# Graph attention and expert layers on one core: the attention's compares and masks run three units ahead of TensorE instead of four

## The reference

```python
seq = (layernorm(x) @ W_seq).reshape(N, H, DH)
score1, score2 = einsum(seq, a1), einsum(seq, a2)          # [H, N] each
scores = leaky_relu(score1[:, :, None] + score2[:, None, :], 0.2)
scores = scores + (1 - adj)[None] * -65500.0
hidden = einsum('hij,jhd->ihd', softmax(scores, -1), seq).reshape(N, 512)
x = x + elu(hidden @ W_out + b_out)
x = x + ffn(layernorm(x))       # shared FFN of 2048, 8 experts, 2 chosen per token
```

## Time and profile before

| | |
|---|---|
| median of 3 runs | 1058.4 us (1056.4 to 1060.9) |
| profiled execution, its own time | 1060.8 us |
| its span, first to last instruction | 1058.9 us |
| attention's units on TensorE | 99.8 to 487.9 us |
| mean granted TensorE clock | 0.983 of full speed |

### The profile page before, as it was taken

One profiled execution on the slowest core, in us unless ns is written; L12 is line 12 of the kernel. 1 busy time (PEld: TensorE's weight loads), 2 busy tenths in 40 slices (PEclk: granted clock), 3 DMA queues, 4 the chain that ended last, 5 costly groups with the idle time before them and its releaser, 6 DMA issues.

```text
span 1058.9 us, 27195 instructions
## 1 busy us (share of the span) xinstructions
PE 1006.7 (95%) x11256; PEld 890.0 (84%) x11256; DVE 803.9 (76%) x1197; ACT 666.5 (63%) x990; POOL 251.5 (24%) x271
## 2 busy tenths in 40 slices
PE   5996889999999999999899999999999999989998
PEld 4875889999999999997677888888888877778887
DVE  6776899999999999993699433448775668975554
ACT  2668999999989889933356333344454546655431
POOL 1103124334333443363331000000065000006500
PEclk9996999999999999999899999999999999999999
DMA  8781111111111111623635000020063124453242
GB/s 301 249 313 40 41 62 43 45 61 42 43 52 52 42 43 52 225 67 132 229 116 208 1 1 1 1 80 1 26 207 117 50 80 131 130 158 112 85 134 99
DMA packets 53778, 102.45 MB, mean 97 GB/s; under 512 B 6161, under 2 KB 26257, under 8 KB 53138
## 3 DMA queue, kind: packets, MB, share of 16 engines
q1 hardware_dynamic: 47666, 82.83, 23.6%
q0 software_dynamic: 3072, 8.39, 2.5%
q10 hardware_dynamic: 2928, 9.57, 2.4%
HBM read 74.69 MB, written 26.08 MB: 95 GB/s over the span
## 4 chain that ended last, share of the span: by engine, by line
PE 47%; issue 2%; DVE 2%; DMA 1%; POOL 1%; ACT 0%; SPq 0%; POOLq 0%; DVEq 0%; ACTq 0%
PE bank L1758 16%; PE bank L1291 16%; PE bank L668 3%; PE bank L1835 2%; PE bank L1786 1%; PE bank L1787 1%; PE bank L1789 1%; DMA xs<-sorted_latent_rows 1%; PE bank L1805 1%; PE bank L1779 1%; PE bank L1743 1%; PE bank L1741 1%; PE bank L665 1%; PE bank L1740 1%; DVE acc_rest L1492 0%
## 5 line engine op out<-in xcount | busy, mean ns | idle before, releaser
L730 ACT ACTIVATE arena<-arena 128x1024 fp8e4<-128x1024 f32 x320 | 336.6, 1136 | 2.5 <-ACT arena L722 1.6
L956 PE MATMUL bank<-arena 128*128 128x132 f16 x4096 | 285.6, 222 | 19.0 <-DVE arena L816 7.6
L956 PEld LDWEIGHTS bank<-arena 128*128 128x128 fp8e4 x4096 | 246.6, 98 | 20.8 <-issue 8.6
L1291 PE MATMUL bank<-xt,up_parts 128*128 128x512 f32 x768 | 186.2, 391 | 0.0
L1758 PE MATMUL bank<-down_parts,h_parts 128*128 128x512 f32 x768 | 184.5, 389 | 0.1
L960 PE MATMUL bank<-arena 128*128 128x66 f16 x4096 | 173.5, 196 | 0.0
L794 DVE TENSOR_SCALAR arena<-arena 128x1024 uint8<-128x1024 f32 x192 | 167.8, 940 | 2.7 <-DMA arena<-s_rows 2.7
L1758 PEld LDWEIGHTS bank<-down_parts,h_parts 128*128 128x128 f32 x768 | 143.9, 188 | 30.5 <-issue 0.5
L1291 PEld LDWEIGHTS bank<-xt,up_parts 128*128 128x128 f32 x768 | 142.3, 188 | 28.6 <-ACT relu_sb L1240 0.2
L960 PEld LDWEIGHTS bank<-arena 128*128 128x128 fp8e4 x4096 | 154.9, 98 | 0.0
L1265 DVE TENSOR_TENSOR relu_sb<-relu_sb 128x512 f32<-128x512 f32 x64 | 44.4, 693 | 118.0 <-ACT relu_sb L1240 110.9
(11 more groups left out here) (231 smaller groups left out, 1403.9 us busy)
## 6 DMA issues: line engine op xcount, KB each, us to landing
hid<-in_adjT SPq DMA_DIRECT2D x32, 512.0 KB, 5.8
arena<-s_rows SPq DMA_DIRECT2D x30, 512.0 KB, 3.7
sorted_latent_rows<-zeros SPq DMA_DIRECT2D x1, 4992.0 KB, 18.5
xs<-sorted_latent_rows SPq DMA_DIRECT2D x39, 128.0 KB, 2.1
sorted_expert_rows<-expert_y SPq DMA_DIRECT2D x39, 128.0 KB, 1.7
arena<-in_x SPq DMA_DIRECT2D x4, 1024.0 KB, 10.8
xr<-in_x SPq DMA_DIRECT2D x16, 256.0 KB, 2.8
up_sb<-in_upT ACTq DMA_DIRECT2D x1, 4096.0 KB, 14.0
```

Source lines behind the costliest of these rows:

```text
L730: last = nc.scalar.activation(m8[:, k, j, :], s1b[:, k % 2, :], ACT.Sigmoid, bias=bias_now[:, k % 2, j:j + 1], scale=STEEP, saturate=False)
L956: last = nc.tensor.matmul(o, m8[:, k, j, i * P:(i + 1) * P], vs[:, b, j, :], start=(j == 0), stop=(j == T - 1))
L1291: last = nc.tensor.matmul(bank[6 + s % 2][:, :], sa[:, s % 2, a, k, :], xt[c][:, b, k, :], start=(i == 0), stop=(i == len(mm) - 1))
```

## The change

`compare`, `mask_own` and `mask_acts` are called one unit closer to TensorE. In the slot of unit u, VectorE and ScalarE compare unit u + 3 and `mask_acts` is that of unit u + 2. Unit 3's compare, which was ahead of the loop, moves into slot 0, and the last pair's slots get the compare of unit 31 and the masks of units 30 and 31. GpSimd's wait on `m_ready` is lowered by one, so that it still means the end of VectorE's slot u - 1. The mask buffers stay four, and no instruction that computes is added or removed.

```diff
@@ ScalarE
                 def body(p, last):
                     for k in range(4):
-                        act.wait_ge(unit_in_psum, 4 * p + k + 1)
-                        if not last:
-                            if k >= 2:
-                                split_high(p + 1, k % 2)
-                            compare(p + 1, k)
+                        if not (last and k):
+                            act.wait_ge(unit_in_psum, 4 * p + k + 1)
+                        if not last and k >= 2:
+                            split_high(p + 1, k % 2)
+                        if not last or k == 0:
+                            compare(p + (k + 3) // 4, (k + 3) % 4)
...
                 compare(0, 2)
-                compare(0, 3)
                 with act.Fori(0, PAIRS - 1) as p:
                     body(p, False)
+                body(PAIRS - 1, True)
@@ VectorE
-                        if k or not first:
-                            dve.wait_ge(unit_in_psum, 4 * p + k + 1)
-                            collect(p, k)
-                        if not last:
-                            if k >= 2:
-                                low_values(p + 1, k % 2)
-                            compare(p + 1, k)
-                            mask_own(p + 1, k)
-
-                        if k == 0:
-                            mask_acts(p, 3)
-                        elif not last:
-                            mask_acts(p + 1, k - 1)
+                        dve.wait_ge(unit_in_psum, 4 * p + k + 1)
+                        collect(p, k)
+                        if not last and k >= 2:
+                            low_values(p + 1, k % 2)
+                        if not last or k == 0:
+                            compare(p + (k + 3) // 4, (k + 3) % 4)
+                            mask_own(p + (k + 3) // 4, (k + 3) % 4)
+                        if not last or k < 2:
+                            mask_acts(p + (k + 2) // 4, (k + 2) % 4)
...
                 mask_own(0, 2)
-                mask_acts(0, 2)
-                dve.wait_ge(unit_in_psum, 1)
-                collect(0, 0)
-                compare(0, 3)
-                mask_own(0, 3)
-                body(0, first=True)
-                with dve.Fori(1, PAIRS - 1) as p:
+                with dve.Fori(0, PAIRS - 1) as p:
                     body(p)
                 body(PAIRS - 1, last=True)
@@ GpSimd
-                        pool.wait_ge(m_ready, 4 * p + k + 3)
+                        pool.wait_ge(m_ready, 4 * p + k + 2)
                         pool.wait_ge(unit_in_psum, 4 * p + k + 1)
```

More of the change, by code:

```diff
@@ L831, in split_low, with body @@
                     nc.vector.tensor_scalar(ones_r[0:1, :], ident2[0:1, :], 0.0, 1.0, ALU.mult, ALU.add).then_inc(wo_low, 1)
-                def body(p, last=False, first=False):
+                def body(p, last=False):
                     for k in range(4):
```

## The result

The changed kernel takes 1075.5 us (median of 4 runs, 1073.7 to 1081.0) against 1059.7 us for the kernel before on the same chip (4 runs). The ratio is 1.016 with a 95% interval of 1.013 to 1.019: 16 us slower. The forecast was 1072.7 us, 14.3 us above before, in a range of 1065 to 1080. The single profiled executions say the same, with spans of 1074.8 and 1058.9 us. From the first matmul of unit 0 to the last `collect` the attention takes 504.12 - 99.31 = 404.8 us against 487.96 - 99.76 = 388.2, and from that `collect` to the end it is 570.7 us against 570.9. So the whole loss is in the attention.

The account below looks back on a forecast made before the run. VectorE was taken as the bound in the attention, TensorE 1% behind. Turns +10.8, start +3.5 and end 0 gave +14.3 us on 1058.4: 1072.7 us, own range 1066 to 1078, stated range 1065 to 1080.

Parts of the forecast that it names:

- The bound, and how much of the lead was left: Attention: VectorE bounds, TensorE 1% behind; masks are ready only 2.2 to 3.4 us before their unit starts.
- The turn as the sum of the larger of slot and unit: Four-slot attention turn: each slot costs the longer of VectorE's slot and TensorE's unit; 48.75 for 46.95 us, +10.8 in six.
- The start: First units of the attention: unit 2's mask comes later, unit 4 ends at 174.4 for 170.9; +3.5 us.
- The end: Behind unit 28: last slots and transposes before unit 31 stay hidden; 0 us, or 1 if it sticks out.
- ScalarE at no cost: Attention turns: ScalarE gets less slack, but its longest slot, 11.4 us, just fits in a unit; cost nothing.
- The clock: TensorE in the turns: priced at no loss; rival: a cold unit once a turn, +9 us, 1081.6 us, chance 0.07.
- The rivals of the slots: VectorE's slots: they even out (1063.4 us, chance 0.10) or GpSimd's interference goes (1056.7 us, chance 0.04).
- evening out: Rival, VectorE's slots become equally long: 1.5 us lost in all turns, with the start +5, 1063.4 us; chance 0.10.
- less interference: Rival, GpSimd's products run in VectorE's waits, compares shorten: turns -5.2, start +3.5, 1056.7 us; chance 0.04.
- the other side's mechanism: Not-slower rival: without GpSimd's interference all slots are under 11.8 us and TensorE runs without pause; 1056.7 us, chance 0.04.

Follow-up runs that it names:

- e3: Changed kernel with VectorE's mask of ScalarE's rows moved directly behind `collect`, ahead of low values and compare; 1063.4 us, 1.004 to the kernel before.
- e6: Changed kernel (lead of three) without GpSimd's multiplications for the values of pairs 1 to 7; 1059.9 us, 1.000 to the kernel before.
- e7: Kernel before (lead of four) without GpSimd's multiplications for the values of pairs 1 to 7; 1055.2 us, 0.995 to the kernel before.
- e5: Changed kernel, but in the first slot alone the mask of unit 2's ScalarE rows comes ahead of `collect`; 1073.7 us, 1.015 to the kernel before.
- e8: Changed kernel with one wait more: GpSimd's combine of unit 27 waits for the end of VectorE's slot 27; 1076.9 us (one run).
- e1: Changed kernel with ScalarE four units ahead as before, VectorE and GpSimd's count three ahead; 1079.4 us, 1.020 to the kernel before.
- e2: Kernel before with ScalarE alone three units ahead, VectorE and GpSimd unchanged; 1060.8 us, 1.002 to the kernel before.
- e11: e3 with the transposes behind unit 31's fifth token tile and GpSimd's slot released by the mask near the slot's start; 1071.6 us, 1.010 to before.

## Why the prediction was right

*The bound, and how much of the lead was left.* Right. What the chain of waits didn't say, the distance between mask and start did: 2.2 to 3.4 us were left of the lead, and a slot later was 7 us or more too late. e3 shows it from the other side, as the mask moved forward inside the slot brings the turn back without the fourth unit.

*The turn as the sum of the larger of slot and unit.* Predicted 48.75 us, measured 48.76. That they agree to 0.01 is luck: the two slots longer than a unit were 0.21 and 0.07 us shorter than forecast (11.84 for 12.05, 13.03 for 13.10), and the two that wait for TensorE took 11.95 and 11.94 us where a release was priced at 11.8. The waits were forecast as 1.43 and 0.37 us on VectorE and as 1.6 and 0.5 on TensorE; they are 1.63, 0.42, 1.77 and 0.6. e6, beside e7, agrees with the rule on other slots. Six turns give +10.9 us.

*The start.* Predicted +3.5 us, with unit 2 ready at 135.3, unit 4's release at 174.4; measured +3.6, with slot 4's start at 174.54 against unit 4's end at 170.9 before, and unit 0 0.45 us sooner. VectorE's timeline of the start in the changed kernel:

```profile
125.44 1.38 DVE L817 TENSOR_REDUCE arena<-bank 128x198 f32<-128x396 f32 x3
...
149.58 1.39 DVE L817 TENSOR_REDUCE arena<-bank 128x198 f32<-128x396 f32 x3 [4.07 <-PE bank L947]
```

Slot 0 starts at 125.44, forecast 125.5, and slot 2 at 149.58 behind a wait of 4.07 us, forecast 149.5. e5 took 2.7 us of this away.

*The end.* This is the term that was mis-sized: 0 to 1 us was allowed, and about 1.6 us came. Slot 27 is not the 11.43 us of its kind:

```profile
455.26 1.38 DVE L817 TENSOR_REDUCE arena<-bank 128x198 f32<-128x396 f32 x3
...
467.86 1.38 DVE L817 TENSOR_REDUCE arena<-bank 128x198 f32<-128x396 f32 x3
```

It takes 12.6 us, since GpSimd's combine behind the loop starts early and slows its compares (shown by e8), so unit 29 waited 0.92 us, to 468.09, instead of following unit 28; a pause of 0.22 us inside a unit, put down to no engine ("issue"), came on top. The trace before had it, with slot 27 from 449.52 to 462.12, and I had not laid that row into the sum. TensorE's timeline accounts for nearly all of it: unit 29 starts 1.1 us later than directly behind unit 28 (the 0.92 us and 0.17 of the last matmul's drain), where it followed directly before, and from its start to the last `collect` it is 36.0 us against 35.6. What stays open are the pauses: e8 took the wait away, and other pauses of the same size appeared. The transposes were hidden, as predicted.

*Sum:* 10.9 + 3.6 + 1.6 = 16.1 us at the attention's end (504.12 against 487.96), and 15.9 between the spans, for a forecast of 14.3. (The forecast's own range left the runs' spread out at its upper end: 18.7 and 2 over 1058.4 is 1079, not 1078.)

*ScalarE at no cost.* Right in the changed kernel, where e1 gives ScalarE its lead back and the turn stays. Its waits in the profile are waits of an engine with time to spare. With VectorE four ahead, ScalarE's lead of three costs 1.4 us (e2), by the wait at the end.

*The clock.* The clock stayed at 1.00 in the turns, so that rival is out. After the pause of 10.57 us it was 0.50; after 2.74 us in e5 it was still 1.00, and after the 3.40 us before unit 3 in the kernel before it was 0.53 (146 to 149 us). The Trainium skill (TensorE: Matmul & The Clock Gate, "A second HAM failure mode: psum-queue depth-cycling") warns that frequent short idling can make the clock swing, and gives no size for it there. The trace does not bear it out here: with pauses of 1.77 and 0.6 us once each a turn the granted clock stood at 1.00 from 200 to 465 us.

*The rivals of the slots.* Neither evening out nor less interference came by itself: the compares kept their times, but for 0.2 us in slot k = 0 (6.10 for 6.30). That the other side's mechanism exists is shown by e6, where the products are left out and the kernel with a lead of three is as fast as before.

## What to carry to other kernels

A wait that never shows in the chain of waits may still have no slack: before a unit is taken off a lead, measure from the moment the buffer is ready to the moment it is used, for every kind of slot, and where the lead only just spans the way from a release through the consumer and back, each slot longer or shorter than a unit is paid for. With a lead this short, put the piece that releases the other engine first in its slot: that brought back 12 of the 16 us here, and with the transposes moved the kernel was 3 to 4 us under the one with the fourth unit of lead, which costs preparation ahead of the first one. With the lead of four the same order lost 5.6 us, since another piece that TensorE waits for came later by it. And whatever starts earlier helps only if all that joins it at the end is early too.

## What the runs showed of the hardware

GpSimd and VectorE disturb each other unevenly. With GpSimd's combine beside a mask (two tensors in) the mask takes 2.89 to 3.12 us instead of 2.82 and the low values 1.70 instead of 1.33, and GpSimd's add 3.00 instead of 1.44 (e3); with combine and products beside the compares (one tensor in) six of them go from 4.07 to 6.1 us. Moving GpSimd by 4 us within the slot (e11) made a turn 2.2 us longer. And after a pause of 3.48 and one of 0.73 us (e3) the granted clock was 0.51 and TensorE took 12.9 us for a unit of 11.7, while one pause of 2.74 us (e5) and pauses of 1.77 us once a turn left it at 1.00.
